# A reordered refill of the projection's right-hand side in an attention and feed-forward kernel on Trainium2

## The chip, the cores and the metric

The kernel runs on one core of a Trainium2 chip. The metric is the device time of one execution in microseconds; the table below gives the median of three runs. The five engines, with the names that the profile gives them, are TensorE (PE, its weight loads PEld), VectorE (DVE), ScalarE (ACT), GpSimd (POOL) and SyncE (SP), which here only issues DMAs. Each engine works through its own queue in order and waits on semaphores that the other engines raise.

## What is computed

```python
def reference(x, itok_B_0_15, itok_B_0_7, ...):
    # x is (64, 64, 1024)
    x = x + attention(condition(x, itok_B_0_15, weights), qkvw, qkvb, ow, ob)
    x = x + ffn(condition2(x, itok_B_0_7, W, Wr, A, B), w_gate, ...)
    return x

def condition(x, condition, weights):         # weights (16, 64, 64)
    W = weights[condition]
    return jnp.einsum('bct,bcd->bdt', x, W)
```

The attention has 32 heads of 32 channels over 64 positions, and its `qkv = x @ qkvw + qkvb` has 4096 rows. Everything is float32 up to the feed-forward part.

## The kernel before, in words

The kernel has three parts in time: the attention stage (condition, projection to q, k and v, scores, softmax, context), up to about 1150 us; the output projection; and the feed-forward stage. The change touches the attention stage alone.

**Blocks and units.** The 4096 rows are four blocks (`BLOCKS`, r) of 1024. A block's projection is 12 units (`UNITS`), so U runs from 0 to 47 over the whole stage. A unit is one step of Strassen's scheme in Winograd's form: 7 products (`SLOTS`, k = 0 to 6) in place of 8. Each product is 12 matmuls (L800): for each of four chunks hi×hi, hi×lo and lo×hi, since each float32 operand is held as a rounded high part and a remainder, the low part. (U, k) below is product k of unit U.

**The refill of y.** A block's right-hand side is made by the condition: four pairs of tiles (`PAIR`, p = 0 to 3), each pair two halves of 8 matmuls into four PSUM banks, `att` for even and `acc` for odd pairs (`y_bank`; the trace shows each of these matmuls as two, so x16 is a half, and the line is L762). From the four quarters Y11, Y12, Y21, Y22 in PSUM a pair needs seven operands, each as high (`y_hi`) and low (`y_lo`). `spot(k, p)` is operand k, pair p.

- ScalarE copies Y11 to a staging tile (L547) and writes the seven highs: 0 and 5 from PSUM (L550, L551), 1 and 2 from `y_raw` (L553, L555), 3 from PSUM (L556), 4 and 6 from `y_raw` (L558, L562).
- VectorE makes the mixed operands in `y_raw`: t1 = Y12 - Y11 (L667, needs the staged copy and the pair's second half), t2 (L671), operand 4 (L673), operand 6 (L677). It also makes the lows 0, 5 and 3 (all L656).
- GpSimd makes the lows 1, 2, 4 and 6 (L428).

This refill takes place four times: before unit 0, and after units 11, 23 and 35. Within a refill every engine goes pair by pair. `raw_at`, `hi_at` and `lo_at` turn "operand k of pair p" into the count of a semaphore, and so depend on the order of each engine. Matmuls of pair p + 2 wait until pair p has left their banks (L746 on). Product 0 after a refill waits for low 0 of pair 3, product k for low k.

**The refill of the weights.** For each unit from 1 on GpSimd makes all seven weight slots (L395 high, L397 low) and four mixed quarters (L400), a unit ahead of TensorE at most. `w_raw` holds the four quarters of one unit; SyncE loads the next (L270) once `w_set` says that GpSimd has split the old. At the last unit of a block GpSimd does its y lows between slot 4 and slot 5 of the next unit's weights.

**What else SyncE has in its queue.** The same queue, in a fixed order by (U, k), holds the transposes of the probabilities (`turn_p`, L312, pv<-pw) and of v (`turn_v`, L318, vv<-vw), the context's stores, and the loads of x for the next refill (L288). ScalarE fetches the transposed tiles (L481, L501) in its own fixed order, between the `unit_out` activations (L529 to L536) that take products out of PSUM; product (U, 4) waits for the one of (U, 2) (L534).

The order around the change is written out by hand in each engine's function:

```python
for U in range(ALL - 1):          # GpSimd
    for k in range(SLOTS):
        if k == 5 and U % UNITS == UNITS - 1:
            for p in range(PAIR):
                refill_y(U // UNITS + 1, p)
        refill_w(U + 1, k)
```

Of the kernel before, what the change touches and what calls it, by code (L numbers as in the profile page):

```python
# [102 lines left out]
def attention_stage(nc, ctx, io, ctxT, ident, banks, link, after):  # L103
# [104 lines left out]
    HIGHS, LOWS_DVE, LOWS_POOL = (0, 5, 1, 2, 3, 4, 6), (0, 5, 3), (1, 2, 4, 6)  # L208
# [167 lines left out]
    def gpsimd(pool):  # L376
# [54 lines left out]
        def refill_y(r, p):  # L431
            n = PAIR * r + p
            pool.wait_ge(t_raw, raw_at(2, n + 1))
            pool.wait_ge(y_hi_set, hi_at(1, n + 1))
            low(1, p)
            pool.wait_ge(t_raw, raw_at(4, n + 1))
            pool.wait_ge(y_hi_set, hi_at(2, n + 1))
            low(2, p)
            pool.wait_ge(y_hi_set, hi_at(4, n + 1))
            low(4, p)  # L440
            pool.wait_ge(y_hi_set, hi_at(6, n + 1))
            low(6, p)

        for p in range(PAIR):
            refill_y(0, p)
        for U in range(ALL - 1):
            for k in range(SLOTS):
                if k == 5 and U % UNITS == UNITS - 1:
                    for p in range(PAIR):
                        refill_y(U // UNITS + 1, p)  # L450
                refill_w(U + 1, k)

    def scalar(act):
# [85 lines left out]
        def refill_y(r, p):  # L539
# [16 lines left out]
            act.activation(y_hi[spot(3, p)], flat(bank[:, Y22]), ACT.Identity).then_inc(y_hi_set, 1)  # L556
# [1497 lines left out]
```

## Time and profile before

| | |
|---|---|
| median of 3 runs | 2138.26 us (2130.25 to 2140.66) |
| profiled execution, its own time | 2137.01 us |
| its span | 2135.2 us |
| PE busy | 2067.5 us (97%) |
| DVE busy | 1433.3 us (67%) |
| POOL busy | 1363.0 us (64%) |
| ACT busy | 1030.7 us (48%) |
| chain that ended last | PE 78%, POOL 12%, DMA 4%, DVE 2%, ACT 2%, issue 2% |

The busy shares are means over the whole span; the chain is the sequence of work and waits followed back from the last instruction. A timeline row gives the start, the duration, the engine, the line of the kernel, the operation with its tiles, and in brackets the idle time before it with what ended that idle time. The profiled execution's time lies 1.8 us over its span and 1.3 us under the median.

### The profile page before, as it was taken

How to read it: one execution, taken by the hardware profiler on the slowest of the kernel's cores; microseconds unless marked ns; L12 is line 12 of the kernel's file. 1: busy time of each engine (PE TensorE's matmuls, PEld its weight loads, DVE VectorE, ACT ScalarE, POOL GpSimd, SP SyncE). 2: the span in 40 equal slices, each digit the busy share in tenths (PEclk: the TensorE clock that was granted, in tenths of full speed). 3: DMA queues.
4: the chain of work that ended last, by engine and by line, in shares of the span. 5: the costliest groups of instructions: out<-in, count | busy, mean ns of one | idle time of the engine just before them, and what ended most of it. 6: DMA issues, size and time to landing. Idle time of an engine off the chain costs nothing.

```text
span 2135.2 us, 45792 instructions
## 1 busy us (share of the span) xinstructions
PE 2067.5 (97%) x17984; PEld 1687.0 (79%) x18016; DVE 1433.3 (67%) x2403; ACT 1030.7 (48%) x1334; POOL 1363.0 (64%) x1137
## 2 busy tenths in 40 slices
PE   6999999999999999999998899999999999999996
PEld 6888878788778888788887788888877777787785
DVE  5355464555565555645556965656799999999998
ACT  4366565565575566655665322223443443344342
POOL 7888888888889888888886800001445444444443
PEclk9999999999999999999999999999999999999998
DMA  3355555555545545445556355367544454444433
GB/s 127 88 107 126 110 142 113 107 119 107 145 121 107 122 109 126 137 96 128 110 129 217 115 193 191 115 198 233 118 123 116 98 122 114 106 115 117 114 94 92
DMA packets 427374, 270.47 MB, mean 127 GB/s; under 512 B 289986, under 2 KB 358722, under 8 KB 426690
## 3 DMA queue, kind: packets, MB, share of 16 engines
q1 hardware_dynamic: 423762, 263.74, 48.8%
q0 software_dynamic: 2864, 3.28, 0.9%
q8 instruction: 121, 1.98, 0.4%
q10 hardware_dynamic: 576, 1.05, 0.1%
q14 instruction: 51, 0.42, 0.1%
HBM read 152.92 MB, written 50.33 MB: 95 GB/s over the span
## 4 chain that ended last, share of the span: by engine, by line
PE 78%; POOL 12%; DMA 4%; DVE 2%; issue 2%; ACT 2%; SPq 0%; POOLq 0%; DVEq 0%; ACTq 0%
PE acc L800 30%; PE acc L1864 16%; PE acc L1222 7%; PE att L1222 7%; POOL w_slot_lo L397 5%; PE att L1897 5%; POOL w_raw L400 3%; PE att L1834 3%; POOL w_slot_hi L395 3%; PE acc L1909 3%; DMA w_raw<-wu 2%; PE att L829 2%; PE acc L1873 2%; PE att L856 2%; DMA x_raw<-x 1%
## 5 line engine op out<-in xcount | busy, mean ns | idle before, releaser
L800 PE MATMUL acc<-y_hi,w_slot_hi 128*128 128x512 f32 x1344 | 532.8, 396 | 13.6 <-issue 7.8
L800 PE MATMUL acc<-y_hi,w_slot_lo 128*128 128x512 f32 x1344 | 525.4, 391 | 0.0
L800 PE MATMUL acc<-y_lo,w_slot_hi 128*128 128x512 f32 x1344 | 525.3, 391 | 0.0
L397 POOL TENSOR_TENSOR w_slot_lo<-w_raw,w_slot_hi 128x512 fp32r<-128x512 f32 x329 | 431.8, 1312 | 26.3
L800 PEld LDWEIGHTS acc<-y_hi,w_slot_hi 128*128 128x128 f32 x1344 | 253.3, 188 | 72.7 <-issue 15.5
L400 POOL TENSOR_TENSOR w_raw<-w_raw 128x512 f32<-128x512 f32 x188 | 252.3, 1342 | 77.7 <-DMA w_raw<-wu 74.0
L800 PEld LDWEIGHTS acc<-y_hi,w_slot_lo 128*128 128x128 f32 x1344 | 253.3, 188 | 53.6
L800 PEld LDWEIGHTS acc<-y_lo,w_slot_hi 128*128 128x128 f32 x1344 | 253.4, 189 | 50.9
L622 DVE TENSOR_REDUCE top<-att 128x8 f32<-128x512 f32 x126 | 86.5, 686 | 252.5 <-PE att L829 246.1
L653 DVE TENSOR_TENSOR unit<-acc,unit 128x512 f32<-128x512 f32 x144 | 99.4, 690 | 219.1 <-PE acc L800 209.7
L395 POOL CAST w_slot_hi<-w_raw 128x512 fp32r<-128x512 f32 x329 | 224.5, 682 | 12.3 <-PE acc L800 0.2
L1864 PE MATMUL acc<-f_w_hi,f_x_hi 128*128 128x512 f32 x512 | 202.6, 396 | 0.4 <-issue 0.4
L1864 PE MATMUL acc<-f_w_hi,f_x_lo 128*128 128x512 f32 x512 | 199.7, 390 | 0.0
L1864 PE MATMUL acc<-f_w_lo,f_x_hi 128*128 128x512 f32 x512 | 199.3, 389 | 0.0
L1462 POOL TENSOR_TENSOR f_x_lo<-f_x_all,f_x_hi 128x1024 fp32r<-128x1024 f32 x32 | 77.1, 2410 | 178.6 <-DVE f_xi L1657 131.9
L481 ACT ACTIVATE prob_T<-pv 128x1024 uint16<-128x1024 uint16 x122 | 159.9, 1370 | 49.7 <-DMA pv<-pw 27.4
L1109 ACT ACTIVATE slot_hi<-c_raw 128x512 fp32r<-128x512 f32 x108 | 62.5, 628 | 215.3 <-DVE c_raw L1153 144.9
L636 DVE TENSOR_TENSOR prob<-prob,inv 128x512 f32<-128x512 f32 x126 | 140.2, 1113 | 4.4
L1222 PE MATMUL acc<-slot_hi,wo 128*128 128x512 f32 x432 | 137.7, 392 | 4.6 <-DVE slot_lo L1158 2.5
L1222 PE MATMUL att<-slot_hi,wo 128*128 128x512 f32 x432 | 136.5, 390 | 3.0 <-DVE slot_lo L1158 3.0
L457 ACT ACTIVATE prob<-prob 128x512 f32<-128x512 f32 x126 | 77.8, 630 | 123.2 <-DVE prob L624 123.1
L475 ACT ACTIVATE pw<-prob 128x1024 uint16<-128x1024 uint16 x122 | 126.4, 1046 | 3.9 <-DVE prob L636 2.6
(205 smaller groups left out, 3890.2 us busy)
## 6 DMA issues: line engine op xcount, KB each, us to landing
w_raw<-wu SPq DMA_DIRECT2D x188, 256.0 KB, 3.2
c_raw<-context_T SPq DMA_DIRECT2D x16, 1024.0 KB, 5.9
f_x_all<-x_T SPq DMA_DIRECT2D x32, 512.0 KB, 4.9
f_xr_all<-x_T SPq DMA_DIRECT2D x32, 512.0 KB, 6.1
out<-f_raw SPq DMA_DIRECT2D x31, 512.0 KB, 3.4
context_T<-cx SPq DMA_DIRECT2D x60, 256.0 KB, 3.2
x_raw<-x SPq DMA_DIRECT2D x27, 512.0 KB, 4.3
xa<-xT SPq DMA_DIRECT2D x12, 1024.0 KB, 7.1
```

The lines of the kernel that those rows point to most:

```text
L395: pool.tensor_copy(w_hi[:, k], raw).then_inc(w_hi_set, 1)
L397: pool.tensor_tensor(w_lo[:, k], raw, w_hi[:, k].bitcast(F32), ALU.subtract).then_inc(w_set, 1)
L400: pool.tensor_tensor(w_raw[:, dst], w_raw[:, a], w_raw[:, b], op).then_inc(w_mix, 1)
L475: act.activation(pw[:, p], words(prob[:, p]), ACT.Copy).then_inc(pw_set, 1)
L481: act.activation(words(prob_T[:, p]), pv[:, p].rearrange("p (h j) n -> p h (j n)", h=2), ACT.Copy)\
L622: dve.tensor_reduce(top[:, p], s3, AX.X, ALU.max).then_inc(top_set, 1)
L636: dve.tensor_tensor(p3, p3, inv[:, p].unsqueeze(2).broadcast_to([P, 8, SEQ]), ALU.mult)\
L653: dve.tensor_tensor(uo[U % 3][:, o], acc[:, a % 2], uo[U % 3][:, o], ALU.add).then_inc(dve_out, 1)
L800: ins = pe.matmul(bank, w[:, k, c, :], v[:, k, c, :], start=(k in (0, 1, 5) and c == 0 and i == 0), stop=(c == C // 2 - 1 and i == 2), ski ...
L1222: ins = pe.matmul(bank, wo[w[j]][:, cols], v[:, c], start=(j < 3 and c == 0 and i == 0), stop=(c == C // 2 - 1 and i == 2), skip_group_che ...
L1864: pe.matmul(z_ps[:, b], a[one][:, c, :], w[:, c, b * HALF:(b + 1) * HALF], start=(c == 0 and k == 0), stop=False)
L1897: ins = pe.matmul(g_ps[:, i], qT[i][:, c], gu_w[:, c, i], start=(c == 0), stop=(c == C - 1))
```

## The change

Three things, all in the refill of y; no instruction is added or removed.

- VectorE does the lows 0 and 5 of a pair ahead of t1, where low 0 stood behind t1 and low 5 behind operand 6.
- ScalarE's refill is cut into a first part (the staged copy, highs 0 and 5), a middle part (highs 1, 2, 3) and a last part (highs 4 and 6). From pair 2 on the first part of a pair stands ahead of the last part of the pair in front of it.
- GpSimd does the lows 1, 2, 4, 6 of pair 0, then 1 and 2 of pairs 1, 2 and 3, then 4 and then 6 of pairs 1 to 3.

The waits are made to fit: `hi_at` and `lo_at` count in the new orders, the matmuls of pair p + 2 wait for low 5 and operand 6 of pair p, and product 0 after a refill waits for t1 of pair 3 as well.

```diff
-    HIGHS, LOWS_DVE, LOWS_POOL = (0, 5, 1, 2, 3, 4, 6), (0, 5, 3), (1, 2, 4, 6)
+    LOWS_DVE = (0, 5, 3)
+    HIGHS = [(k, p) for p, ks in ((0, (0, 5, 1, 2, 3, 4, 6)), (1, (0, 5, 1, 2, 3)), (2, (0, 5)), (1, (4, 6)),
+                                  (2, (1, 2, 3)), (3, (0, 5)), (2, (4, 6)), (3, (1, 2, 3, 4, 6))) for k in ks]
+    LOWS_POOL = [(k, 0) for k in (1, 2, 4, 6)] + [(k, p) for p in (1, 2, 3) for k in (1, 2)] \
+        + [(k, p) for k in (4, 6) for p in (1, 2, 3)]
...
+            for k, p in LOWS_POOL:
+                n = PAIR * r + p
+                if k < 3:
+                    pool.wait_ge(t_raw, raw_at(2 * k, n + 1))
+                pool.wait_ge(y_hi_set, hi_at(k, n + 1))
+                low(k, p)
...
+        def refill_y(r):
+
+            refill_first(r, 0)
+            refill_middle(r, 0)
+            refill_last(r, 0)
+            refill_first(r, 1)
+            refill_middle(r, 1)
+            for p in range(2, PAIR):
+                refill_first(r, p)
+                refill_last(r, p - 1)
+                refill_middle(r, p)
+            refill_last(r, PAIR - 1)
...
             t1, t2 = y_raw[spot(1, p)], y_raw[spot(2, p)]
+            if r and p == 0:
+                dve.wait_ge(prod_mm, SLOTS * (UNITS * r - 1) + 6)
+            dve.wait_ge(y_hi_set, hi_at(0, n + 1))
+            low(0, p, bank[:, Y11])
+            dve.wait_ge(y_hi_set, hi_at(5, n + 1))
+            low(5, p, bank[:, Y21])
             dve.wait_ge(y_mm, 2 * n + 2)
             dve.wait_ge(r11_set, n + 1)
-            if r and p == 0:
-                dve.wait_ge(prod_mm, SLOTS * (UNITS * r - 1) + 6)
             dve.tensor_tensor(t1, flat(bank[:, Y12]), flat(stage(r)[:, p % 2]), ALU.subtract).then_inc(t_raw, 1)
-            dve.wait_ge(y_hi_set, hi_at(0, n + 1))
-            low(0, p, bank[:, Y11])
             dve.wait_ge(t_raw, raw_at(1, n + 1))
             dve.tensor_tensor(t2, flat(bank[:, Y22]), t1, ALU.subtract).then_inc(t_raw, 1)
             dve.wait_ge(t_raw, raw_at(2, n + 1))
             dve.tensor_tensor(y_raw[spot(4, p)], t2, flat(bank[:, Y11]), ALU.subtract).then_inc(t_raw, 1)
-            dve.wait_ge(y_hi_set, hi_at(5, n + 1))
             if r and p == 0:
                 dve.wait_ge(prod_mm, SLOTS * (UNITS * r - 1) + 7)
             dve.tensor_tensor(y_raw[spot(6, p)], flat(bank[:, Y21]), t2, ALU.subtract).then_inc(t_raw, 1)
-            low(5, p, bank[:, Y21])
             dve.wait_ge(y_hi_set, hi_at(3, n + 1))
             low(3, p, bank[:, Y22])
...
             if p > 1 and half == 0:
-                pe.wait_ge(y_lo_dve, lo_at(0, n - 1))
-                pe.wait_ge(t_raw, raw_at(3, n - 1))
                 pe.wait_ge(y_lo_dve, lo_at(5, n - 1))
+                pe.wait_ge(t_raw, raw_at(4, n - 1))
...
-                if k == 1:
-                    pe.wait_ge(t_raw, raw_at(3, PAIR * (r + 1)))
+                if k < 2:
+                    pe.wait_ge(t_raw, raw_at((1, 3)[k], PAIR * (r + 1)))
```

ScalarE's queue before, from the middle part of pair 1 to the staged copy of pair 3 (`att` is pair 2's bank, `acc` that of pairs 1 and 3):

```order
L553 ACTIVATE y_hi<-y_raw 128x4x128
L555 ACTIVATE y_hi<-y_raw 128x4x128
L556 ACTIVATE y_hi<-acc 128x4x128
L558 ACTIVATE y_hi<-y_raw 128x4x128
L562 ACTIVATE y_hi<-y_raw 128x4x128
L547 ACTIVATE unit<-att 128x512
L550 ACTIVATE y_hi<-att 128x4x128
L551 ACTIVATE y_hi<-att 128x4x128
L553 ACTIVATE y_hi<-y_raw 128x4x128
```

The same stretch now, with the changed kernel's line numbers (L551 is the staged copy, L554 and L555 highs 0 and 5, L560, L562 and L563 highs 1, 2 and 3, L568 and L572 highs 4 and 6):

```order
L560 ACTIVATE y_hi<-y_raw 128x4x128
L562 ACTIVATE y_hi<-y_raw 128x4x128
L563 ACTIVATE y_hi<-acc 128x4x128
L551 ACTIVATE unit<-att 128x512
L554 ACTIVATE y_hi<-att 128x4x128
L555 ACTIVATE y_hi<-att 128x4x128
L568 ACTIVATE y_hi<-y_raw 128x4x128
L572 ACTIVATE y_hi<-y_raw 128x4x128
L560 ACTIVATE y_hi<-y_raw 128x4x128
```

The staged copy and highs 0 and 5 of pair 2 moved ahead of highs 4 and 6 of pair 1.

VectorE's queue before, one pair (pair 3, from t1 to the lows 5 and 3):

```order
L667 TENSOR_TENSOR y_raw<-acc,unit 128x4x128
L656 TENSOR_TENSOR y_lo<-acc,y_hi 128x4x128
L671 TENSOR_TENSOR y_raw<-acc,y_raw 128x4x128
L673 TENSOR_TENSOR y_raw<-y_raw,acc 128x4x128
L677 TENSOR_TENSOR y_raw<-acc,y_raw 128x4x128
L656 TENSOR_TENSOR y_lo<-acc,y_hi 128x4x128 x2
```

The same pair now (L677 is a low, L692 t1, L694 t2, L696 and L699 operands 4 and 6):

```order
L677 TENSOR_TENSOR y_lo<-acc,y_hi 128x4x128 x2
L692 TENSOR_TENSOR y_raw<-acc,unit 128x4x128
L694 TENSOR_TENSOR y_raw<-acc,y_raw 128x4x128
L696 TENSOR_TENSOR y_raw<-y_raw,acc 128x4x128
L699 TENSOR_TENSOR y_raw<-acc,y_raw 128x4x128
L677 TENSOR_TENSOR y_lo<-acc,y_hi 128x4x128
```

Two lows stand ahead of t1, one behind operand 6. GpSimd's sixteen lows are one line of code before and after, and differ only in which operand and pair each takes.

## Rows read from the trace of the kernel before

**Rows 1.** Waits of GpSimd, 33 to 1150 us: total us, times, longest us.
```profile
POOL w_slot_hi L395 <- PE acc L800: 0.2, 1, 0.2
```

**Rows 2.** Timeline, first refill, pair 2 into pair 3.
```profile
28.33 0.68 DVE L671 TENSOR_TENSOR y_raw<-att,y_raw 128x512 f32<-128x512 f32 x1
29.04 0.63 ACT L555 ACTIVATE y_hi<-y_raw 128x512 fp32r<-128x512 f32 x1 [0.53 <-DVE y_raw L671]
29.04 0.69 DVE L673 TENSOR_TENSOR y_raw<-y_raw,att 128x512 f32<-128x512 f32 x1
29.58 0.58 ACT L556 ACTIVATE y_hi<-att 128x512 fp32r<-128x512 f32 x1
30.06 0.62 ACT L558 ACTIVATE y_hi<-y_raw 128x512 fp32r<-128x512 f32 x1
...
31.10 0.59 ACT L547 ACTIVATE unit<-acc 128x512 f32<-128x512 f32 x1
31.57 0.60 ACT L550 ACTIVATE y_hi<-acc 128x512 fp32r<-128x512 f32 x1
31.78 0.69 DVE L667 TENSOR_TENSOR y_raw<-acc,unit 128x512 f32<-128x512 f32 x1 [0.26 <-ACT unit L547]
32.39 0.68 DVE L656 TENSOR_TENSOR y_lo<-acc,y_hi 128x512 fp32r<-128x512 f32 x1
32.99 0.68 DVE L671 TENSOR_TENSOR y_raw<-acc,y_raw 128x512 f32<-128x512 f32 x1
33.22 0.76 PE L800 MATMUL acc<-y_hi,w_slot_hi 128*128 128x512 f32 x1 [3.00 <-DVE y_lo L656]
```

**Rows 3.** Timeline, GpSimd's lows in the first and the second refill.
```profile
19.77 19.88 POOL L428 TENSOR_TENSOR y_lo<-y_raw,y_hi 128x512 fp32r<-128x512 f32 x16 [7.41 <-DVE y_raw L671]
...
304.52 15.49 POOL L428 TENSOR_TENSOR y_lo<-y_raw,y_hi 128x512 fp32r<-128x512 f32 x12 [3.45 <-DVE y_raw L671]
```

**Rows 4.** Timeline, t1 of pair 1 in the second and the third refill.
```profile
302.55 0.69 DVE L667 TENSOR_TENSOR y_raw<-acc,unit 128x512 f32<-128x512 f32 x1 [4.09 <-PE acc L762]
...
591.46 0.69 DVE L667 TENSOR_TENSOR y_raw<-acc,unit 128x512 f32<-128x512 f32 x1 [3.34 <-PE acc L762]
```

**Rows 5.** The chain that ended last, unit 16: start us, us, what.
```profile
406.99 1.30 POOL w_slot_lo L397
...
408.73 3.92 DMA pv<-pw
...
413.92 0.66 ACT unit L534
...
414.72 8.41 PE acc L800 x36
```

**Rows 6.** Timeline, weight slot 4 and product 4 of units 4 and 25.
```profile
116.79 1.28 POOL L397 TENSOR_TENSOR w_slot_lo<-w_raw,w_slot_hi 128x512 fp32r<-128x512 f32 x1
...
130.10 0.39 PE L800 MATMUL acc<-y_hi,w_slot_hi 128*128 128x512 f32 x1
...
628.79 1.28 POOL L397 TENSOR_TENSOR w_slot_lo<-w_raw,w_slot_hi 128x512 fp32r<-128x512 f32 x1
...
638.04 0.39 PE L800 MATMUL acc<-y_hi,w_slot_hi 128*128 128x512 f32 x1
```

**Rows 7.** Timeline, weight slot 6 of unit 11, and the second refill's first matmuls.
```profile
273.78 1.29 POOL L397 TENSOR_TENSOR w_slot_lo<-w_raw,w_slot_hi 128x512 fp32r<-128x512 f32 x1
...
289.92 3.77 PE L762 MATMUL att<-wc_raw,x_raw 128*128 128x128 f32 x32
```

**Rows 8.** The chain, from weight slot 6 of unit 23 to the third refill.
```profile
564.64 1.31 POOL w_slot_lo L397
...
573.91 3.81 DMA x_raw<-x
...
577.87 4.23 PE att L762 x21
```

**Rows 9.** The first matmuls after the first refill: us, busy us of each engine, granted clock, DMA share, GB/s.
```profile
33.20:39.40 6.20, 6.18 (x15) 4.84 (x16) 2.96 (x5) 2.78 (x5) 6.20 (x6) 0.51 0.02 4
```

More of the change, by code:

```diff
@@ L214, in hi_at @@
     def hi_at(k, pairs):
-        return SLOTS * (pairs - 1) + HIGHS.index(k) + 1
+        r, p = divmod(pairs - 1, PAIR)
+        return len(HIGHS) * r + HIGHS.index((k, p)) + 1
     def lo_at(k, pairs):
-        return 3 * (pairs - 1) + LOWS_DVE.index(k) + 1 if k in LOWS_DVE else 4 * (pairs - 1) + LOWS_POOL.index(k) + 1
+        if k in LOWS_DVE:
+            return 3 * (pairs - 1) + LOWS_DVE.index(k) + 1
+        r, p = divmod(pairs - 1, PAIR)
+        return len(LOWS_POOL) * r + LOWS_POOL.index((k, p)) + 1
     def before(U, k):
@@ L429, in low @@
                 .then_inc(y_lo_pool, 1)
[L431 to L445, printed above, removed]
+        def refill_y(r):
[5 more added lines that the diff above has]
+                low(k, p)
+        refill_y(0)
         for U in range(ALL - 1):
@@ L448, in gpsimd @@
                 if k == 5 and U % UNITS == UNITS - 1:
-                    for p in range(PAIR):
-                        refill_y(U // UNITS + 1, p)
+                    refill_y(U // UNITS + 1)
                 refill_w(U + 1, k)
@@ L537, in unit_out, with refill_first @@
                     .then_inc(act_out, 1)
-        def refill_y(r, p):
+        def refill_first(r, p):
             n = PAIR * r + p
@@ L551, in refill_y, with refill_middle @@
             act.activation(y_hi[spot(5, p)], flat(bank[:, Y21]), ACT.Identity).then_inc(y_hi_set, 1)
+        def refill_middle(r, p):
+            n = PAIR * r + p
             act.wait_ge(t_raw, raw_at(1, n + 1))
@@ L555, in refill_y, with refill_last @@
             act.activation(y_hi[spot(2, p)], y_raw[spot(2, p)], ACT.Identity).then_inc(y_hi_set, 1)
-            act.activation(y_hi[spot(3, p)], flat(bank[:, Y22]), ACT.Identity).then_inc(y_hi_set, 1)
+            act.activation(y_hi[spot(3, p)], flat(y_bank(p)[:, Y22]), ACT.Identity).then_inc(y_hi_set, 1)
+        def refill_last(r, p):
+            n = PAIR * r + p
             act.wait_ge(t_raw, raw_at(3, n + 1))
@@ L562, in refill_y @@
             act.activation(y_hi[spot(6, p)], y_raw[spot(6, p)], ACT.Identity).then_inc(y_hi_set, 1)
+        def refill_y(r):
+            refill_first(r, 0)
[8 more added lines that the diff above has]
+            refill_last(r, PAIR - 1)
         def first_high(k, reg):
@@ L573, in scalar @@
             first_high(k, reg)
-        for p in range(PAIR):
-            refill_y(0, p)
+        refill_y(0)
         act.wait_ge(small_in, 32)
@@ L601, in scalar @@
             if U % UNITS == UNITS - 1 and U + 1 < ALL:
-                for p in range(PAIR):
-                    refill_y(U // UNITS + 1, p)
+                refill_y(U // UNITS + 1)
         unit_out(ALL - 1, SLOTS - 1)
```

## The prediction

> **What bounds the kernel.** I went from the stage as a whole to the four refills and then to what couples GpSimd to TensorE. In the attention stage TensorE's products follow each other almost without a gap, so there are two kinds of time to win or lose: the idle time in a refill, and whatever makes a product wait later on.
>
> In a refill the reader should follow one loop [rows 2]. t2 (L671) of pair 2 starts at 28.33; ScalarE's high 2 starts 0.71 later, high 3 0.54 after that, high 4 0.48 later, then high 6 and the next pair's staged copy, 1.04 on, at 31.10; t1 follows 0.68 after the copy, low 0 0.61 later, t2 0.60 later, at 32.99. One turn is 4.66 us. TensorE stands idle for 3.00 us at its end, and product 0 starts 0.83 after low 0.
>
> GpSimd is the second thing to see. Once the lows of pair 1 are open it has no gap left: sixteen lows in 19.88 us in the first refill, twelve in 15.49 us in the second, 1.24 and 1.29 each [rows 3]. Behind them come the weights of the next unit, and from 33 to 1150 us GpSimd waits for TensorE's products 0.2 us in all [rows 1]. So time that GpSimd loses in a refill stays with it through the block.
>
> That reaches TensorE over SyncE. In the chain of waits [rows 5] GpSimd ends weight slot 4 of unit 16 at 408.29; only then does SyncE get past the load that waits for it, and starts the transpose behind it (408.73, landed at 412.65); ScalarE fetches that tile, then takes product 2 out (413.92), and product 4 starts at 414.72, after a wait. From GpSimd's slot to product 4 that is 6.4 us. I call this distance the lead. It is 6.4 where TensorE waits; in unit 4 it is 130.10 - 118.07 = 12.0, in unit 25 638.04 - 630.07 = 8.0, and no wait shows there [rows 6]. The places are units 4, 7, 10 and so on: one unit in three. Units 13 and 37, the first such places of blocks 2 and 4, have a lead of 6.5 in the same timeline.
>
> **The change, step by step.** Instructions and durations stay; only orders change.
>
> *The loop.* From pair 2 on the staged copy and high 0 come ahead of highs 4 and 6, which takes 1.04 - 0.48 off the way to the copy; but low 0, low 5 and t1 now stand in this order in front of t2. The turn is: 0.71 to high 2, 0.54 to high 3, 0.48 to the copy, 0.47 to high 0, 0.68 to low 0 (as from the copy to t1), 0.60 to low 5, 0.60 to t1, and 0.71 to t2, which needs t1's result (as L673 needs L671's). That is 4.79 us, 0.13 more than 4.66: ScalarE's high 0 is still behind high 3, which VectorE's t2 releases.
>
> *First refill.* For pairs 0 and 1 ScalarE's order is as before, so nothing is gained there: from the copy of pair 1 to t2 it takes 0.47 + 0.68 + 0.60 + 0.60 + 0.71 = 3.06 in place of 0.68 + 0.61 + 0.60 = 1.89, 1.17 later. With two turns of +0.13 and 0.06 from pair 0, t2 of pair 3 starts 1.5 later, at 34.5. Product 0 waits for t1 (0.71 ahead of t2, +0.83) rather than for low 0: 34.6, **+1.4 us**.
>
> *Refills two to four.* In the second and third t1 of pair 1 waited 4.09 and 3.34 us for TensorE's second half [rows 4]; lows 0 and 5, which need only the first half, fit in that wait. What remains: in pair 0 highs 4 and 6 come 0.7 later (two VectorE steps of 0.60 in front of t1, half of them hidden), between them stands the activation that frees the bank for pair 1, so TensorE's pair 1 starts 0.7 later. In the second and fourth refill that is absorbed by a wait for x: 0.3 is left, the two longer turns. In the third it isn't: 0.8 + 0.3. The bounds are 0 and the first refill's 1.4 for each. Taken: **+0.3, +1.1, +0.3**.
>
> *GpSimd.* It now does only lows 1 and 2 of pairs 1 to 3 as they open, 2.6 us of work in a turn of 4.8, and stands idle 2.2 us in each of two turns; the six lows 4 and 6 come after. Low 1 of pair 3 starts about 0.75 after t2 of pair 3 (my estimate from ScalarE's 0.71), and eight lows are left from there, against four before: the end is 34.5 + 0.75 + 8 × 1.26 = 45.4 in the first refill, before 19.77 + 19.88 = 39.65: 5.7 later, 4.3 more than product 0. In the second it is t2 at 313.4, so 313.4 + 0.75 + 8 × 1.29 = 324.5 against 320.0: 4.4 later, 4.1 more than product 0. Products 1, 2 and 4 find their lows in time: low 1 of pair 3 is ready at about 36.6 and 315.5, product 1 starts no earlier than 37.3 and 316.3. Nothing is gained from GpSimd's order, since no product waited for a low other than low 0.
>
> *What the lag costs.* Where the lead covers it, nothing. Block 1: 12.0 - 4.3 = 7.7, over 6.4: nothing in its units. Block 2: lead 6.5, so the full 4.1. Block 3: 8.0 - 4.0 = 4.0, under 6.4 by **2.4**. Block 4: like block 2, **4.1**. Once TensorE has waited, it stands to GpSimd as before and the rest of the block only shifts. At a block's end GpSimd waits 2.5 to 3.5 us for t2 of pair 0, so little lag is carried on.
>
> *The loads of x.* At the end of block 2 weight slot 6 of unit 23 is done at 565.95, the x load goes out 8.0 us later at 573.91, behind two transposes, and TensorE starts at 577.87 having waited [rows 8]. At the end of block 1 slot 6 is done at 275.07 and TensorE starts at 289.92 without a wait [rows 7]. With GpSimd 5.7 later the load goes out at 280.8 + 8.0 = 288.8 and lands, as 573.91 did, 4.0 later at 292.8; TensorE wants it at 291.3. **+1.5**, bounds 0 and 3.2 (it may start slow, as the third refill's did). At the end of block 3 the lag left is under 2 and is covered.
>
> *The clock.* After the 3.00 us of idle time the granted clock was 0.51 for 6.2 us [rows 9], that is 1.2 GHz, and 15 matmuls stood where some 27 fit. After the second and fourth refill's shorter gaps it stayed at 2.4 GHz; those gaps grow to about 3.3 and 3.0. If the clock falls there too, product 4 comes up to 2.8 us later, but it was going to wait 4.1 for GpSimd's lag: I cost it at nothing, and 2.8 each if that cover is gone. The Trainium skill (TensorE: Matmul & The Clock Gate, Part 1) says that an idle array falls back to 4 of 8 clock pulses and gets the rest back only after sustained work. By that rule the two longer gaps would start at half clock and, without the lag, the sum would be 5.6 higher; with it, unchanged.
>
> **Sum**: 1.4 + 1.5 + (0.3 + 4.1) + (1.1 + 2.4) + (0.3 + 4.1) = 15.2 us. The profiled execution's own time is 2137.0, so 2152.2; it lies 1.3 under the median of the runs, and I forecast **2152.5**.
>
> **Rivals.**
>
> *The lag is absorbed.* If the 6.4 of lead isn't a floor (say SyncE's order leaves the transposes room that unit 16 doesn't show), only the refills' own terms remain: 1.4 + 0.3 + 1.1 + 0.3 = 3.1, perhaps 1.5 for x: **2141 to 2143**. Against it: the chain of waits runs through GpSimd for most of blocks 2 and 4. Chance 0.25.
>
> *The lag costs more.* With less lead everywhere SyncE's loads of weights go out later too and GpSimd's own waits grow; or the clock falls where no wait covers it. One more floor of 4 us in block 1 and 2.8 of clock once or twice: **2157 to 2162**. Chance 0.15.
>
> *The other side: VectorE's turn decides.* If highs 0 and 5 are always ready, a turn is VectorE's own work, 5 × 0.60 + 2 × 0.71 = 4.42, 0.24 under 4.66. Three turns in four refills give 2.9 us, and if the shorter gap keeps the clock at 2.4 GHz after the first refill, 2.8 more; product 0 then comes early, and if the lag is absorbed as well the time is **2132**. It decides only if ScalarE gets from t2 to the next high 0's result in less than VectorE's three steps behind t2 (1.9); by the rows it takes 0.71 + 0.54 + 0.48 + 0.47 + 0.68 = 2.9. Chance 0.05.
>
> *The change does not do as it says*: the order of instructions shows that it does.
>
> **How the numbers follow.** Forecast 0.55, the others 0.25, 0.15 and 0.05. 0.5% is 10.7 us, about what a measurement of this kernel can tell from no change. The forecast's own range is 2147 to 2158, and a tenth of its chance lies under 2149. Slower by over 0.5%: 0.15 + about 0.48 of the 0.55 = 0.63. Faster by over 0.5%: 0.03, the far part of the last rival. The rest, 0.34, is within 0.5%. The range 2139 to 2161 leaves out most of the last rival and the far ends of the first two.
>
> **What would show it.** Right: a turn of 4.8 us in the refills; product 0 at about 34.6; GpSimd's lows of the first refill in pieces with two gaps of 2.2 us and an end near 45.4; TensorE waiting 4 us in front of product 4 of unit 13 and of unit 37 and 2 to 3 in unit 25, each ended by ScalarE's activation, with slot 4 about 6.4 us ahead; a wait for x of about 1.5 us in the second refill. Wrong: turns under 4.66; no wait at unit 13 although GpSimd's slots are 4 us later; waits of products for their own weight slots; or GpSimd's lows without a gap.

## The result, and the profile after

| | before | after |
|---|---|---|
| median of 6 runs each, side by side, us | 2136.86 (2130.25 to 2141.41) | 2154.59 (2149.83 to 2155.27) |
| ratio of the times | 1 | 1.0086 [1.0068, 1.0103] |
| profiled execution, us | 2137.01 | 2155.15 |
| its span, us | 2135.2 | 2153.5 |
| granted TensorE clock, mean | 0.993 | 0.988 |

The change makes the kernel slower by 17.7 us between the medians and 18.3 between the spans. The forecast was 2152.5, 15.2 us more than the profiled execution before.

The page of the changed kernel, busy time and the chain's shares by engine:

```profile
PE 2078.7 (97%) x18016; PEld 1694.3 (79%) x18016; DVE 1435.0 (67%) x2403; ACT 1032.1 (48%) x1334; POOL 1362.8 (63%) x1137
...
PE 78%; POOL 11%; DVE 4%; DMA 3%; ACT 2%; issue 2%; SPq 0%; POOLq 0%; DVEq 0%; ACTq 0%
```

GpSimd is busy 63% of the span and holds 11% of the chain (12% before). The mean hides where: in the page's 40 slices it is busy 70% or more in every one but the first up to 1130 us, and hardly at all from 1240 to 1500 us.

The timeline of the changed kernel, first refill to product 0, then unit 13, and the other places that the text uses (start us, us, engine, line, operation; in brackets the idle time before it and what ended it):

```profile
26.00 2.60 POOL L437 TENSOR_TENSOR y_lo<-y_raw,y_hi 128x512 fp32r<-128x512 f32 x2 [0.74 <-DVE y_raw L694]
...
30.00 0.69 DVE L694 TENSOR_TENSOR y_raw<-att,y_raw 128x512 f32<-128x512 f32 x1
...
30.77 2.60 POOL L437 TENSOR_TENSOR y_lo<-y_raw,y_hi 128x512 fp32r<-128x512 f32 x2 [2.17 <-DVE y_raw L694]
...
32.21 0.60 ACT L554 ACTIVATE y_hi<-acc 128x512 fp32r<-128x512 f32 x1
...
32.84 1.29 DVE L677 TENSOR_TENSOR y_lo<-acc,y_hi 128x512 fp32r<-128x512 f32 x2 [0.24 <-ACT y_hi L554]
...
34.05 0.68 DVE L692 TENSOR_TENSOR y_raw<-acc,unit 128x512 f32<-128x512 f32 x1
...
34.77 0.69 DVE L694 TENSOR_TENSOR y_raw<-acc,y_raw 128x512 f32<-128x512 f32 x1
...
34.88 0.77 PE L820 MATMUL acc<-y_hi,w_slot_hi 128*128 128x512 f32 x1 [3.68 <-DVE y_raw L692]
...
35.54 10.07 POOL L437 TENSOR_TENSOR y_lo<-y_raw,y_hi 128x512 fp32r<-128x512 f32 x8 [2.18 <-DVE y_raw L694]
...
123.90 1.30 POOL L406 TENSOR_TENSOR w_slot_lo<-w_raw,w_slot_hi 128x512 fp32r<-128x512 f32 x1
...
131.61 0.47 PE L820 MATMUL acc<-y_hi,w_slot_hi 128*128 128x512 f32 x1
...
350.71 1.29 POOL L406 TENSOR_TENSOR w_slot_lo<-w_raw,w_slot_hi 128x512 fp32r<-128x512 f32 x1
...
352.03 0.33 SPq L279 DMA_DIRECT2D w_raw<-wu  x1
...
352.80 1.26 SPq L321 DMA_TRANSPOSE pv<-pw  x1
...
356.22 1.36 ACT L484 ACTIVATE prob_T<-pv 128x1024 uint16<-128x1024 uint16 x1 [2.40 <-DMA pv<-pw]
...
357.44 0.65 ACT L537 ACTIVATE unit<-acc,bias 128x512 f32<-128x512 f32 x1
...
358.24 0.77 PE L820 MATMUL acc<-y_hi,w_slot_hi 128*128 128x512 f32 x1 [3.91 <-POOL w_slot_lo L406]
```

In the refill, VectorE's t2 (L694) of pairs 2 and 3 stands 4.77 us apart; low 0 and low 5 (L677, two at 32.84) are now in front of t1 (L692) and t2, and product 0 follows t1 by 0.83. GpSimd's one piece of sixteen lows [rows 3] is now broken: two lows, a gap of 2.17, two lows, a gap of 2.18, then eight that end at 45.61. Each later refill has the same two gaps of 2.2.

In unit 13 the rows repeat the path of unit 16 before [rows 5]: GpSimd ends weight slot 4 at 352.00, SyncE issues the load that waited for it at 352.03 and the transpose behind that load at 352.80, ScalarE fetches the tile at 356.22 and takes product 2 out at 358.09, and product 4 starts at 358.24 after 3.91 us of idle time. The trace names a weight slot of GpSimd as the releaser only because another of its slots, of the same unit, ended in nearly the same moment (358.20); slot 4 had long been done, and ScalarE's activation ended 0.15 before the matmul.

The waits of TensorE in the changed kernel, 33 to 1150 us: total us, times, longest.

```profile
PE acc L820 <- DVE y_raw L692: 9.9, 4, 3.7
PE acc L820 <- POOL w_slot_lo L406: 7.7, 2, 3.9
PE acc L820 <- ACT unit L537: 5.9, 3, 4.1
...
PE att L782 <- DMA x_raw<-x: 2.6, 1, 2.6
```

The second and third lines together (13.6 us) are all waits in front of product 4: 3.91 in unit 13, 3.75 in unit 25, 4.13 in unit 37, and 0.9 and 0.8 in units 7 and 10. Before, the longest such wait was 1.11, in unit 16; now the three long ones come in the second unit of their blocks.

Stretches of the changed kernel: us, busy us of each engine, granted clock, DMA share, GB/s.

```profile
319.90:326.10 6.20, 6.15 (x27) 5.14 (x28) 4.93 (x7) 6.11 (x10) 5.58 (x5) 1.00 0.22 42
...
358.20:364.40 6.20, 6.16 (x15) 4.87 (x16) 1.35 (x2) 3.10 (x3) 4.44 (x5) 0.51 0.71 150
...
649.30:655.50 6.20, 6.20 (x17) 4.93 (x18) 1.34 (x2) 3.06 (x3) 4.42 (x4) 0.59 0.72 149
...
940.30:946.50 6.20, 6.20 (x20) 4.94 (x21) 1.34 (x2) 3.05 (x3) 4.19 (x4) 0.72 0.67 133
```

The last three begin where product 4 starts after each wait. The clock is at its lower level for all or part of them, and 15, 17 and 20 matmuls stand where 27 do at full clock (first line, product 0 of unit 12, behind 1.85 us of idle time). At 0.227 us a matmul (6.20 / 27.3) that is 2.8 + 2.3 + 1.7 = 6.8 us on top of the waits. The starts of products 5 and 6 give about the same: 2.9, 2.5 and 1.6 us beyond the wait.

How much later each place is than before, and what the forecast had for the stretch between (first matmul of the product named, one trace of each kernel). A stretch can differ by 1.5 us for another reason: block 1 is 1.2 to 1.6 shorter than before's in the traces of seven kernels below, mostly because behind the first refill TensorE left the lower clock sooner there.

| stretch | forecast | measured | of what the measured consists |
|---|---|---|---|
| first refill, to (0, 0) | +1.4 | +1.7 | one turn of 5.8 and two of 4.8, where three of 4.66 were |
| block 1, to (11, 5) | 0 | +2.5 | products later by 0.3, 0.2, 1.0 and 1.0 in units 4, 6, 7 and 10 |
| to (12, 0) | +1.8 | +2.5 | the wait for x is 2.58; the clock stays full behind it |
| block 2, to (23, 5) | +4.1 | +4.0 | wait 3.75 more than before, clock 2.8, less some 2.5 that before waited later |
| to (24, 0) | +1.1 | -1.7 | before's wait for x and slow start of the refill are gone (-3.8); the rest is +2.1 |
| block 3, to (35, 5) | +2.4 | +4.7 | wait 3.9 by the starts, clock 2.5, less 1.6: before starts at (24, 0) at the lower clock |
| to (36, 0) | +0.3 | +1.4 | ScalarE's activation in front of pair 1 comes 0.7 later (2.19 for 1.46), two turns 0.2; the rest isn't separated |
| block 4, to (46, 6) | +4.1 | +4.4 | wait 3.9 more than before, clock 1.6, less 1.1 that before waited later |
| to the end | 0 | -1.3 | not of the change: other traces differ by -2.5 to +1.5 there |
| sum | 15.2 | 18.2 | |

### The profile page after: what moved, and what is told of

It reads as the page before. It is cut to its first block, busy times and chain, and to the rows that moved or that the text cites. A ratio compares the mean times of both kernels' runs of the same rounds, so it can differ in the third digit from the quotient of the medians.

```text
span 2153.5 us, 45826 instructions
## 1 busy us (share of the span) xinstructions
PE 2078.7 (97%) x18016; PEld 1694.3 (79%) x18016; DVE 1435.0 (67%) x2403; ACT 1032.1 (48%) x1334; POOL 1362.8 (63%) x1137
## 4 chain that ended last, share of the span: by engine, by line
PE 78%; POOL 11%; DVE 4%; DMA 3%; ACT 2%; issue 2%; SPq 0%; POOLq 0%; DVEq 0%; ACTq 0%
PE acc L820 31%; PE acc L1884 16%; PE att L1242 7%; PE acc L1242 6%; PE att L1917 5%; POOL w_slot_lo L406 4%; PE att L1854 3%; POOL w_raw L409 3%; PE acc L1929 3%; PE att L849 2%; POOL w_slot_hi L404 2%; PE acc L1893 2%; PE att L876 2%; POOL y_lo L437 2%; DMA w_raw<-wu 2%
## 5 line engine op out<-in xcount | busy, mean ns | idle before, releaser
L820 PEld LDWEIGHTS acc<-y_hi,w_slot_hi 128*128 128x128 f32 x1344 | 254.6, 189 | 83.9 <-issue 13.6
L409 POOL TENSOR_TENSOR w_raw<-w_raw 128x512 f32<-128x512 f32 x188 | 250.0, 1330 | 76.1 <-DMA w_raw<-wu 68.8
```

What stands on the lines that cost most here:

```text
L409: pool.tensor_tensor(w_raw[:, dst], w_raw[:, a], w_raw[:, b], op).then_inc(w_mix, 1)
L820: ins = pe.matmul(bank, w[:, k, c, :], v[:, k, c, :], start=(k in (0, 1, 5) and c == 0 and i == 0), stop=(c == C // 2 - 1 and i == 2), ski ...
```

## The experiments

The theory was the prediction's: GpSimd's new order opens two gaps of 2.2 us in each refill, GpSimd has no time to make them good, and SyncE's in-order queue hands the lag to TensorE. The first rival was that the refill's own longer turn (low 0 and low 5 in front of t1) makes the loss. Later ones are named where they came up. Every ratio is against the kernel before, run beside it.

### GpSimd's order alone

The kernel before with GpSimd's part of the change and nothing else (the table is shown; GpSimd's loop goes through it as in the change):

```diff
-    HIGHS, LOWS_DVE, LOWS_POOL = (0, 5, 1, 2, 3, 4, 6), (0, 5, 3), (1, 2, 4, 6)
+    HIGHS, LOWS_DVE = (0, 5, 1, 2, 3, 4, 6), (0, 5, 3)
+    LOWS_POOL = [(k, 0) for k in (1, 2, 4, 6)] + [(k, p) for p in (1, 2, 3) for k in (1, 2)] \
+        + [(k, p) for k in (4, 6) for p in (1, 2, 3)]
```

> GpSimd's new order alone; VectorE and ScalarE as before. Theory (GpSimd's lag is what costs): turn stays 4.66 us, product 0 of unit 0 stays at about 33.2, GpSimd idles about 2.0 us twice in each refill and ends its lows 4 us later (near 43.7 in the first refill); TensorE then waits 4 us in front of product 4 of units 13 and 37 and 1.5 to 4 in unit 25. Slower by 11 to 17 us, 2148 to 2154. Rival (the longer turn in the refill is what costs): slower by less than 3 us.

Measured: 2154.01 us (2148.94 to 2161.01), ratio 1.009 [1.0068, 1.0113], at the upper edge of the theory's range. Its timeline, GpSimd's lows of the first refill, product 0, and product 4 of unit 13:

```profile
20.01 7.53 POOL L433 TENSOR_TENSOR y_lo<-y_raw,y_hi 128x512 fp32r<-128x512 f32 x6 [7.64 <-DVE y_raw L670]
...
29.33 2.60 POOL L433 TENSOR_TENSOR y_lo<-y_raw,y_hi 128x512 fp32r<-128x512 f32 x2 [1.79 <-DVE y_raw L670]
...
33.46 0.77 PE L799 MATMUL acc<-y_hi,w_slot_hi 128*128 128x512 f32 x1 [3.00 <-DVE y_lo L655]
33.99 10.12 POOL L433 TENSOR_TENSOR y_lo<-y_raw,y_hi 128x512 fp32r<-128x512 f32 x8 [2.07 <-DVE y_raw L670]
...
355.68 0.77 PE L799 MATMUL acc<-y_hi,w_slot_hi 128*128 128x512 f32 x1 [4.25 <-ACT unit L533]
```

Product 0 starts at 33.46, 0.24 from where it did before (33.22), and the turn is 4.66 as before. The gaps of 1.79 and 2.07 and the wait of 4.25 in unit 13 are there all the same, this time with ScalarE's activation as its releaser; unit 25 waits 4.0 and unit 37 2.4. One part of the change, which shortens no path and lengthens none that TensorE waits on in the refill, makes the whole loss.

### GpSimd's order undone

The changed kernel with the old order on GpSimd:

```diff
-    LOWS_POOL = [(k, 0) for k in (1, 2, 4, 6)] + [(k, p) for p in (1, 2, 3) for k in (1, 2)] \
-        + [(k, p) for k in (4, 6) for p in (1, 2, 3)]
+    LOWS_POOL = [(k, p) for p in range(4) for k in (1, 2, 4, 6)]
```

> The changed kernel with GpSimd's old order. Theory: turn stays 4.77 and product 0 of unit 0 at 34.9, GpSimd has almost no gap from pair 1 on and ends near 41.5; no wait over 1.5 us in units 13, 25, 37. Slower than the kernel before by 3 to 7 us, 2140 to 2144. Rival (the turn costs): 2151 to 2155, like the whole change.

Measured: 2140.62 us (2137.41 to 2144.92), ratio 1.0025 [1.0013, 1.0038], about 5.4 us over before. Its timeline, GpSimd's lows of the first refill:

```profile
20.52 5.07 POOL L436 TENSOR_TENSOR y_lo<-y_raw,y_hi 128x512 fp32r<-128x512 f32 x4 [8.14 <-DVE y_raw L693]
...
26.32 2.60 POOL L436 TENSOR_TENSOR y_lo<-y_raw,y_hi 128x512 fp32r<-128x512 f32 x2 [0.73 <-DVE y_raw L693]
...
29.45 12.44 POOL L436 TENSOR_TENSOR y_lo<-y_raw,y_hi 128x512 fp32r<-128x512 f32 x10 [0.53 <-ACT y_hi L567]
```

GpSimd ends at 41.89 in place of 45.61, no product waits in unit 13, units 25 and 37 wait 0.2 at most, and product 0 still starts at 35.2. All this is as forecast, and so is the time. What is left isn't all turn: product 4 of unit 28 waits 2.0 in this trace, and product 4 of unit 43 0.96. So ScalarE's and VectorE's orders together cost what is left, and GpSimd's order the rest; the two don't add up (17.7 together, against 0.009 × 2134.5 = 19 and 5.4 each alone). A reason for that, argued and not measured by itself: a product that starts later is also a product that waits less for GpSimd.

### SyncE's loads one product later

If the in-order queue is what couples them, the wait in unit 13 must go when SyncE issues the transpose ahead of the load that waits for GpSimd:

```diff
-                    if k == 4:
+                    if k == 5:
                         load_w(U + 2, R11)
-                    elif k == 5:
+                    elif k == 6:
                         load_w(U + 2, R21)
-                    elif k == 6 and U % UNITS == UNITS - 1:
+                    if k == 6 and U % UNITS == UNITS - 1:
```

On the changed kernel:

> The changed kernel with SyncE's loads of quarters R11 and R21 one product later, behind the transposes of the probabilities and not ahead of them. Theory (GpSimd's lag reaches TensorE through SyncE's queue): GpSimd's lag stays, with slot 4 of unit 13 done 3 to 6 us ahead of its product, but the waits of 4 us at product 4 of units 13, 25 and 37 are gone and the slow clock behind them too (7 us), and the 2.6 us in units 4, 7 and 10: 2133 to 2141. Rival (TensorE waits for its own weight slots, as the profile's releaser says): the waits stay, 2152 to 2157.

On the kernel before:

> The kernel before with the same move in SyncE's queue. Theory: the small waits at product 4 of units 13, 16, 19, 22, 37 and 40 (3.7 us in all) go, nothing else changes: 2132 to 2136. Rival (later loads lengthen GpSimd's own waits for the weights, and it falls behind): 2137 to 2145.

Measured: 2154.8 us (2153.17 to 2161.56), ratio 1.0091 [1.0072, 1.0109], on the changed kernel, and 2136.23, ratio 1.0005 [0.999, 1.0019], on the one before. The edited changed kernel, unit 13 in its timeline:

```profile
346.48 1.24 SPq L321 DMA_TRANSPOSE pv<-pw  x1
...
348.02 1.29 POOL L406 TENSOR_TENSOR w_slot_lo<-w_raw,w_slot_hi 128x512 fp32r<-128x512 f32 x1
...
353.37 0.39 PE L820 MATMUL acc<-y_hi,w_slot_hi 128*128 128x512 f32 x1
```

and its waits, 33 to 1150 us:

```profile
PE att L782 <- DMA x_raw<-x: 9.1, 3, 4.3
...
PE acc L782 <- DMA x_raw<-x: 3.1, 3, 1.1
```

The transpose goes out 1.5 us before slot 4's low starts, not 0.8 after its end, and product 4 starts without a wait with a lead of 4.1 (353.37 - 349.31). That shows the mechanism: 6.4 is no property of GpSimd and TensorE but of the queue between them. But the total, forecast at 2133 to 2141, did not move; it lies where the rival had it, though the waits that the rival wanted are gone. By the traces the four blocks are 11.7 us shorter than in the changed kernel, and the refills 9.1 longer: from product 5 of a block's last unit to product 0 of the next block it takes 29.9, 30.6 and 32.5 us, against 28.7, 27.5 and 27.6. (The other 2.7 come behind the attention stage and have no cause that was found.) A wait gives TensorE's lead over GpSimd back; without it the lag is kept to the end of the block, where the loads of x stand in the same queue behind GpSimd's last slots. TensorE waits for x there three times, 9.1 us in all, where the changed kernel waited once, 2.6, and each time starts the refill at a granted clock of 0.68 for 5.4 us. Taking a wait away moved it.

On the kernel before the time is within noise of no change, just over the theory's 2132 to 2136. Its trace shows the same exchange: no product 4 waits any more, and the fourth refill waits 4.1 us for its first x, where before it waited for none.

### ScalarE's order alone, VectorE's order alone

The two other parts of the change, each on the kernel before (the highs by the new table, or low 0 and low 5 in front of t1).

> ScalarE's new order alone; VectorE and GpSimd as before. By the loop that the prediction used, t2 to the next t2 needs only 0.71 + 0.54 + 0.48 + 0.68 + 0.61 + 0.60 = 3.6 us, so VectorE's own work decides, about 4.4: turns of pairs 2 and 3 of 4.4 in place of 4.66, product 0 0.5 us earlier in each refill, GpSimd ending no later. 2132 to 2137, not to be told from the kernel before. Rival (ScalarE's order by itself delays the highs that GpSimd's lows 4 and 6 need, and so makes the lag): GpSimd's lows end 2 us or more later, waits at units 13, 25, 37, 2140 or more.

> VectorE's new order alone. The loop becomes 0.71 + 0.54 + 1.04 + 0.48 + 0.47 + 0.68 + 0.60 + 0.60 + 0.71 = 5.8 us a turn: product 0 of unit 0 at 36.5 to 36.8, the other refills 2.3 to 3.4 later. GpSimd's end moves with product 0, so there is no lag between them. Theory (a late product 0 costs its own delay and no more): 2143 to 2148. Rival (each microsecond of a refill is paid again in the block): 2152 or more.

Measured: ScalarE's order alone 2139.63 us, ratio 1.0027 [1.0009, 1.0044]; VectorE's order alone 2146.26 us, ratio 1.0052 [1.0031, 1.0073]. With ScalarE's order alone the turn is 4.31 (VectorE's t2 at 28.14 and 32.45), shorter than the 4.66 of before, and product 0 starts at 32.67, 0.55 earlier. It still loses, where the theory had no change: highs 4 and 6 now come behind the next pair's first ones, GpSimd, which needs them, ends its lows at 40.16, 0.5 later, and is 1.0 closer to TensorE at product 0. Its trace has waits of 1.1 and 0.9 in front of product 4 of units 28 and 34, and 3.6 for x in the fourth refill. The rival had the direction right and the size not (2 us). With VectorE's order alone the time is in the theory's range, the turn is 5.80 (t2 at 30.93 and 36.73) and product 0 starts at 36.84, 3.6 later; GpSimd ends at 42.6, 3.0 later, so the lead grows and no product 4 waits. The two hold each other up: ScalarE's order takes 1.0 us off the turn that VectorE's order makes longer.

### More of SyncE's loads moved

A rival to the lag as such: SyncE's queue is badly ordered for every lag, and with all of a unit's loads behind its transposes both kernels gain.

```diff
+                if k == 1 and U and U + 1 < ALL:
+                    load_w(U + 1, R12)
+                    load_w(U + 1, R22)
...
-                    elif k == 6:
-                        load_w(U + 2, R12)
-                        load_w(U + 2, R22)
-                    if k == 1 and U and U % UNITS == 0:
-                        load_w(U + 1, R12)
-                        load_w(U + 1, R22)
```

with the first edit of SyncE's as well, on the kernel before and on the changed one.

> The kernel before, with all four loads of the next weights moved behind the transposes in SyncE's queue: R11 and R21 one product later, R12 and R22 three products later. Theory: TensorE no longer waits at products 4 of blocks 2 and 4 (3.7 us) nor for x in the third refill (2 us and 1.7 of slow clock): 2128 to 2133. Rival: GpSimd waits longer for its weights and falls behind in lead: 2136 or more.

> The changed kernel with the same moves of all four loads. Theory (SyncE's queue carries all of the lag to TensorE, in the last experiment by the loads of x): no wait over 1 us at product 4 of any unit, the waits for x in refills 2 to 4 under 2.5 us each (they were 3.9, 4.6 and 5.9 over the activation's wait): 2136 to 2144. Rival (GpSimd itself is late): waits of 2 us or more for weight slots or for GpSimd's loads, 2150 or more.

Measured: 2166.76 us, ratio 1.0152 [1.0128, 1.0176], and 2186.96 us, ratio 1.0235 [1.021, 1.0259]. The waits of GpSimd, 33 to 1150 us, in the first of them:

```profile
POOL w_raw L397 <- DMA w_raw<-wu: 107.6, 44, 5.7
```

Before, that line had 74.0 us. The loads come later, GpSimd starves, and the lead shrinks from the other end: at product 4 it is 2.4 to 5.0 late in each block, the waits there add up to 12.3 us (2.7 before) and those for x to 17.5 (4.0 before). The queue couples both ways: loads ahead of the transposes carry GpSimd's lag to TensorE, loads behind them make GpSimd lag. The forecast gain was wrong in both kernels, and both times lie in the rivals' ranges.

### Lows moved from GpSimd to VectorE

If lead is what counts, lows that GpSimd doesn't have to do should be worth more than any order. First on the changed kernel, the six lows 4 and 6 of pairs 1 to 3 behind VectorE's refill; then on the kernel before, only (6, 2), (4, 3) and (6, 3); then that with ScalarE's new order. The edit for three lows, without the waits that go with it:

```diff
+    LOWS_POOL = [(k, p) for p in (0, 1) for k in (1, 2, 4, 6)] + [(1, 2), (2, 2), (4, 2), (1, 3), (2, 3)]
+    LOWS_LATE = [(6, 2), (4, 3), (6, 3)]
...
+        def late_lows(r):
+            for k, p in LOWS_LATE:
+                dve.wait_ge(y_hi_set, hi_at(k, PAIR * r + p + 1))
+                dve.tensor_tensor(y_lo[spot(k, p)], y_raw[spot(k, p)], y_hi[spot(k, p)].bitcast(F32), ALU.subtract)\
+                    .then_inc(y_lo_dve, 1)
...
                 for p in range(PAIR):
                     refill_y(U // UNITS + 1, p)
+                late_lows(U // UNITS + 1)
```

> The changed kernel, but the six late lows (4 and 6 of pairs 1 to 3) go from GpSimd to VectorE, which does them behind its own refill. The turn stays 4.77 and product 0 at 34.9, GpSimd ends its lows near 38 in the first refill in place of 45.6. Theory (lag costs, the turn costs only itself): no waits at products 4, none for x in the third refill; 2130 to 2140, that is 15 to 25 us under the changed kernel. Rival (VectorE's 3.6 us more behind the refill delay the softmax and so TensorE by as much): 2145 or more.

> The kernel before, but three lows (6 of pair 2, 4 and 6 of pair 3) go from GpSimd to VectorE behind its refill. GpSimd ends 3.3 us earlier in each refill: lead 9.8 in place of 6.5 at unit 13. Theory: the waits at product 4 (3.7 us in all) and the wait for x with its slow clock in the third refill (3 us) go: 2127 to 2132. Rival (GpSimd's lead is worth nothing to the kernel before): 2134 to 2138.

> The same three lows on VectorE, with ScalarE's new order on top: the turn is 4.31 (measured with that order alone), product 0 0.5 us earlier in each refill, and GpSimd keeps a lead of about 9. Theory (with the lead given, a shorter turn pays): 2125 to 2131, 1 to 3 us under the run without ScalarE's order. Rival (ScalarE's order costs by something else than GpSimd's lead): 2134 or more.

Measured: six lows on the changed kernel 2148.77 us, ratio 1.0063 [1.0041, 1.0086]; three on the kernel before 2141.59, ratio 1.0034 [1.002, 1.0049]; with ScalarE's order 2140.14, ratio 1.0026 [1.0009, 1.0043]. All three miss their theories. The first lies some 5 us under the changed kernel by the two ratios, whose intervals overlap, and not the forecast 15 to 25. Its rival, that the softmax is delayed, is what its timeline shows at the start of block 2:

```profile
316.69 7.85 DVE L712 TENSOR_TENSOR y_lo<-y_raw,y_hi 128x512 fp32r<-128x512 f32 x6
...
328.07 0.47 PE L839 MATMUL acc<-y_hi,w_slot_hi 128*128 128x512 f32 x1 [1.79 <-ACT unit L540]
```

The six lows, taken at 3.6 us in the expectation, took 7.85. ScalarE's `pw` waits for the softmax, the activation behind it, which product 3 needs, comes late, and TensorE waits 1.8 us there and 3.4 in each of the two next blocks.

The second loses where a gain was forecast. The third is inconclusive: it doesn't differ from the second by more than the intervals, and both keep waits in the first units of a block. The timeline of the second, start of block 2:

```profile
315.33 3.52 DVE L690 TENSOR_TENSOR y_lo<-y_raw,y_hi 128x512 fp32r<-128x512 f32 x3
...
316.68 1.62 POOL L408 TENSOR_TENSOR w_slot_lo<-w_raw,w_slot_hi 128x512 fp32r<-128x512 f32 x1
...
317.39 6.25 SPq L323 DMA_TRANSPOSE pv<-pw  x2
...
321.32 1.06 ACT L480 ACTIVATE pw<-prob 128x1024 uint16<-128x1024 uint16 x1 [3.56 <-DVE prob L641]
...
323.69 1.06 SPq L281 DMA_DIRECT2D w_raw<-wu  x2
...
328.15 1.31 POOL L411 TENSOR_TENSOR w_raw<-w_raw 128x512 f32<-128x512 f32 x1 [5.08 <-DMA w_raw<-wu]
```

It reads from top to bottom. VectorE's three late lows delay the softmax, ScalarE's `pw` waits 3.56 us for it, the second transpose stands in SyncE's queue for `pw`, the loads behind it go out at 323.69, and GpSimd waits 5.08 us for them. In the kernel before the same two loads went out 1.7 us earlier, and GpSimd waited 1.38:

```profile
321.96 2.23 SPq L270 DMA_DIRECT2D w_raw<-wu  x2
```

The lead at product 5 of unit 12 is 11.5 as wanted (7.2 before), and at product 4 of unit 13 it is 6.4 (6.5 before): the gain was handed back through the same queue. This execution was the fastest of its kernel (2136.28 against a median of 2141.59), so the trace shows why nothing is gained, and not where the loss comes from.

### The same three lows later, and two loads ahead of the transposes

Two edits follow from that reading, on the kernel with three late lows: VectorE does them at product 2 of the block's first unit, and SyncE's two loads of that unit come ahead of its transposes.

```diff
+                if k == 1 and U and U % UNITS == 0:
+                    load_w(U + 1, R12)
+                    load_w(U + 1, R22)
                 for p in range(2):
...
-                    if k == 1 and U and U % UNITS == 0:
-                        load_w(U + 1, R12)
-                        load_w(U + 1, R22)
...
+                if k == 2 and U % UNITS == 0:
+                    late_lows(U // UNITS)
```

> The last but one kernel (three lows on VectorE, everything else as before) with two repairs. VectorE does the three lows in product 2 of the unit, behind the softmax that the trace showed them delaying by 2.4 us, and SyncE issues the two loads for unit 13 (25, 37) ahead of the transpose that the trace showed them waiting behind for 3.6 us. Theory (GpSimd's lead was gained in the refill and lost again at these loads): the mixed quarter of unit 13 starts near 324.5 in place of 328.2, lead at unit 13 near 10, no waits at products 4: 2127 to 2132. Rival (the lead is lost elsewhere): 2135 to 2142.

Measured: **2127.55 us** (2125.55 to 2132.55, 11 runs), ratio **0.9971 [0.9959, 0.9984]**; before, beside it, 2132.63. The gain is 0.3%, small but clear of the interval, and in the theory's range. Its timeline at the same place:

```profile
318.69 3.81 DVE L690 TENSOR_TENSOR y_lo<-y_raw,y_hi 128x512 fp32r<-128x512 f32 x3
...
319.42 1.87 SPq L281 DMA_DIRECT2D w_raw<-wu  x2
321.39 1.53 SPq L323 DMA_TRANSPOSE pv<-pw  x1
...
324.51 1.28 POOL L411 TENSOR_TENSOR w_raw<-w_raw 128x512 f32<-128x512 f32 x1 [0.88 <-DMA w_raw<-wu]
```

The loads go out 4.3 us earlier and GpSimd waits 0.88 rather than 5.08. The lead at product 4 of units 4, 13, 16, 25, 28, 37 and 40 is 12.3, 10.3, 11.5, 9.4, 10.7, 7.2 and 8.2, over 6.4 everywhere, and no product 4 waits. This is the fastest of all kernels here, by the two ratios some 25 us under the changed one, and it goes the opposite way: it gives GpSimd less to do in a refill, and ahead of pair 3's lows GpSimd waits 0.3 to 0.9 us and not 2.2. The two edits were made together; what each gives, and what SyncE's edit alone would give the kernel before, was not measured.

## Why the prediction was right, and where its steps were not

**The loop, the first refill, GpSimd: right.** The turn was forecast at 4.79 us and is 4.77, product 0 at 34.6 and is at 34.88, GpSimd's gaps at 2.2 (2.17 and 2.18) and its end at 45.4 (45.6).

**That the lag reaches TensorE: right, and shown.** GpSimd's order alone makes the loss, its undoing takes some 13 us away (1.0086 to 1.0025), and the waits stand in units 13, 25 and 37 as forecast. The rival that the lag is absorbed falls with them; the one that VectorE's turn decides falls with the turn. One premise was read from too little: that time lost by GpSimd stays lost was taken from its waits for TensorE (0.2 us), but it also waits 74.0 us for the loads of its weights. They gave little back: 68.8 in the changed kernel. (The wait for t2 of pair 0, "2.5 to 3.5", is 3.7 in the second refill.)

**"Block 1: nothing in its units": failed.** The step took the lag at the refill (4.3) off the lead of unit 4 (12.0) and had 7.7. The timeline gives 131.61 - 125.20 = 6.4, at the floor: slot 4 is 7.1 us later than before, where GpSimd's lows end 6.0 later. The lag grows on the way. From slot 4 of unit 1 to slot 4 of unit 4 GpSimd took 64.3 us where it took 63.2, of which 0.8 more in waits for the loads of weights and 0.3 in its own instructions; by unit 10 slot 4 is 10.9 later. TensorE then waits in four units, and the block is 2.5 longer. That is the first half of the rival "the lag costs more": GpSimd's own waits grow with it.

**The clock "costed at nothing": failed.** I had looked for a fall after the refills' gaps, where I took them to grow to about 3.3 and 3.0; they measured 1.85 and 2.20, and the clock stayed full behind them. What I left out is that the new waits of 4 us are idle time too. The clock fell behind each, 6.8 us in all. This is the other half of the same rival.

**"The rest of the block only shifts": failed, in the other direction.** TensorE loses the clock's 2.8 us as well as the wait, GpSimd works on, and behind the wait of unit 13 the lead is 9 to 13. The waits of before in units 16, 19 and 22 do not come back. Block 2 is 4.0 longer, as forecast, but by a wait of 3.75 and 2.8 of clock less some 2.5 that before spent later. The sum of the block was right by two errors of that size that nearly cancel, which is luck.

**The wait for x: right in place, short in size**, 2.58 for 1.5: slot 6 of unit 11 is 9.1 later and not 5.7. **Third refill: failed.** Forecast +1.1, measured -1.7: with TensorE later and the lead at 11 rather than 6.6 the wait of before [rows 8] was gone, and with it the slow start of the refill, 3.8 in all; the rest of the refill is 2.1 longer, not 1.1. **Fourth refill:** +1.4 for +0.3, by 0.7 of the activation that was taken to be hidden there.

**Block 3: short by 2.3.** The wait was forecast at 2.4 and is 3.9, because the lag isn't 4.0 but 5.5: slot 4 of unit 25 is 12.9 later, TensorE only 7.4, since it no longer starts (24, 0) at the lower clock. That gives 1.6 back in the same block, and the clock behind the wait adds 2.5.

So the sum, 15.2 for 18.2, is close in part by luck. Left out on one side were 6.8 of clock, 2.5 in block 1, 1.5 of the wait in unit 25 and 1.1 each at x and in the fourth refill; on the other the waits that did not come back, the third refill, and the slow clock of before at (24, 0). The mechanism, and the places where it shows, were as forecast.

## What to carry to other kernels

An engine that is busy two thirds of the time can still have little slack in the stretch that counts; an order that leaves it idle there while it waits for the most urgent operand can cost the idle time later (here two gaps of 2.2 us in a refill came back as a wait of 4 in three blocks). Before a step is moved, follow every in-order queue that the engine shares with others by a load that waits for it, and write down the lead at each such place, not the waits alone: a wait shows where lead has run out, and nothing of where it is about to. And a wait that vanishes is no gain until the next item in the queue has been looked at; here SyncE's first edit, in both kernels, turned waits for ScalarE into waits for x, and the three late lows moved them from units 16 and 22 to units 25 and 28.

## What the runs showed of the hardware

**The clock falls after a wait of 4 us in mid-block, and that adds four to seven tenths of the wait to it.** Behind 3.91 us of idle time the granted clock was 0.51 for 6.2 us, the lower level of 1.2 GHz, worth 2.8 us; behind 3.75 and 4.13 it was 0.59 and 0.72, worth 2.3 and 1.7. Idle time alone doesn't order the cases: before, product 0 of unit 24 started behind 2.48 us, and 602 to 608 had a clock of 0.72; product 0 of unit 36 started behind 2.58, and 886 to 892 had 1.00. The refill that waited 1.99 us for x in the run with SyncE's loads one product later had 0.68 for 5.4 us; the one that waited 2.58 in the changed kernel kept 1.00. The Trainium skill's rule that the prediction weighed (TensorE: Matmul & The Clock Gate, Part 1: an idle array falls back to half its pulses) agrees with the three waits of 4 us; these 2.58, and the 1.85 and 2.20 of the changed kernel's refills, show that not every idle stretch does it. What decides is not shown here: ahead of unit 24 the clock had been full from 584 to 600.

**VectorE and GpSimd slow each other on lows whose operands are both in SBUF.** A low of VectorE with one operand in PSUM takes a step of 0.60 [rows 2], beside GpSimd too. In the run with three late lows on the kernel before, the same three lows with both operands in SBUF took 2.00 us in the first refill (at 36.43, with GpSimd idle for 1.38 of them) and 3.52 in the second, beside GpSimd, whose own low there took 1.62 in place of 1.29. So SBUF operands alone don't make them slow. The Trainium skill (SBUF — State Buffer, section "SBUF: two separate sides") says that such a VectorE instruction takes a port pair that it shares with GpSimd, for the whole instruction, and that the other blocks meanwhile. The rows agree: a single low of VectorE took 0.68 us alone and up to 1.78 beside GpSimd, that is 1.10 more, less than one of GpSimd's instructions of 1.29; GpSimd's low grew by 0.33, less than one of VectorE's of 0.68.
